# Last stage: first logits of the next group ahead of tree 7's masks, LN4's rows a tree earlier, and GpSimd makes LN3's rows

## The reference, cut to what matters

```python
x = x + _L0_xattn_ref(_layernorm(x), ctx, W, b)
x = x + _L0_ffn_ref(_layernorm(x), ...)          # shared part + one expert of 8 per token
x = x + _L1_xattn_ref(_layernorm(x), ctx, ctx, Wq, bq, Wk, bk, Wv, bv)     # LN3
x = x + _L1_ffn_ref(_layernorm(x), W_in, b_in, W_out)                      # LN4

def _L1_ffn_ref(oldx, W_in, b_in, W_out):        # 8 trees of 255 nodes
    logits = x @ W_in.T + b_in
    decisions = logits > 0
    acts = silu(logits)
    # from the root, the decision at each node picks one of its two children, 7 levels deep
    # dmap is 1 at the 8 nodes on that path, 0 elsewhere
    return (acts * dmap) @ W_out.T
```

## Time and profile before

| | us |
|---|---|
| median of 3 runs | 847.22 (845.65 to 848.89) |
| the profiled execution | 849.45 |
| its span, first to last instruction | 847.6 |
| third stage in it | from 365.8 to the end |
| TensorE busy | 787.2 (93%) |
| VectorE busy | 655.7 (77%) |
| ScalarE busy | 541.6 (64%) |
| GpSimd busy | 265.4 (31%) |

### The profile page before, as it was taken

One profiled execution on the slowest core, in us unless ns is written; L12 is line 12 of the kernel. 1 busy time (PEld: TensorE's weight loads), 2 busy tenths in 40 slices (PEclk: granted clock), 3 DMA queues, 4 the chain that ended last, 5 costly groups with the idle time before them and its releaser, 6 DMA issues.

```text
span 847.6 us, 15269 instructions
## 1 busy us (share of the span) xinstructions
PE 787.2 (93%) x4452; PEld 633.5 (75%) x4493; DVE 655.7 (77%) x1742; ACT 541.6 (64%) x948; POOL 265.4 (31%) x308
## 2 busy tenths in 40 slices
PE   5899998987878998999999999999999999999997
PEld 4788776776768898977777777777777777777775
DVE  5888889787844456768988887888888788888774
ACT  3577667565322334366877777777777777778765
POOL 2333222887287143112320321232132133111000
PEclk9999999999999999999999999999999999999999
DMA  6346784742334343100000000000000000000000
GB/s 170 89 137 191 194 221 130 202 130 85 87 108 149 95 116 91 51 26 13 26 23 4 25 25 0 25 25 19 6 25 25 0 25 25 11 14 14 14 1 25
DMA packets 91428, 55.88 MB, mean 66 GB/s; under 512 B 13439, under 2 KB 88055, under 8 KB 91255
## 3 DMA queue, kind: packets, MB, share of 16 engines
q1 hardware_dynamic: 75440, 41.29, 17.4%
q0 software_dynamic: 4096, 8.40, 3.5%
q10 hardware_dynamic: 11847, 5.64, 2.4%
HBM read 32.23 MB, written 23.07 MB: 65 GB/s over the span
## 4 chain that ended last, share of the span: by engine, by line
PE 41%; DVE 28%; issue 12%; ACT 12%; POOL 3%; another core or an unknown queue 2%; DVEq 1%; DMA 0%; ACTq 0%; POOLq 0%; SPq 0%
PE PS L823 7%; PE PS L808 6%; DVE sil_l L1522 4%; DVE dec L1506 3%; DVE xn_c L1149 3%; PE PS L1009 3%; PE PS L1068 3%; PE PS L1069 3%; PE PS L1070 3%; ACT sil L765 3%; DVE xn L1149 2%; PE PS L1090 2%; PE PS L1092 2%; PE PS L1091 2%; DVE st L1138 2%
## 5 line engine op out<-in xcount | busy, mean ns | idle before, releaser
L765 ACT ACTIVATE sil<-PS,b_in_c 128x512 f32<-128x512 f32 x256 | 162.3, 686 | 113.6 <-PE PS L1077 71.3
L1522 DVE TENSOR_TENSOR sil_l<-sil,sil_h 128x512 fp32r<-128x512 f32 x256 | 164.8, 685 | 44.7 <-ACT sil_h L773 44.3
L526 POOL TENSOR_TENSOR ve<-mv,eps 128x4 f32<-128x4 f32 x64 | 19.2, 300 | 450.2 <-DVE mv L1143 450.1
L773 ACT ACTIVATE sil_h<-sil 128x512 fp32r<-128x512 f32 x224 | 128.9, 631 | 0.0
L1090 PE MATMUL PS<-sil_h,wout_l 128*128 128x512 f32 x256 | 117.8, 460 | 1.6 <-DVE sil_l L1522 1.6
L1506 DVE TENSOR_SCALAR dec<-PS,b_in_c 128x512 bf16<-128x512 f32 x128 | 95.6, 747 | 26.1 <-PE PS L1070 24.3
L1068 PE MATMUL PS<-x4T_h,win_l 128*128 128x512 f32 x256 | 102.2, 399 | 1.6 <-ACT yo L725 0.7
L1092 PE MATMUL PS<-sil_h,wout_h 128*128 128x512 f32 x256 | 100.8, 394 | 0.0
L1091 PE MATMUL PS<-sil_l,wout_h 128*128 128x512 f32 x256 | 100.3, 392 | 0.0
L1069 PE MATMUL PS<-x4T_l,win_h 128*128 128x512 f32 x256 | 100.0, 390 | 0.0
L1070 PE MATMUL PS<-x4T_h,win_h 128*128 128x512 f32 x256 | 99.8, 390 | 0.0
(11 more groups left out here) (169 smaller groups left out, 1549.6 us busy)
## 6 DMA issues: line engine op xcount, KB each, us to landing
x_sorted<-zeros SPq DMA_DIRECT2D x4, 1280.0 KB, 6.8
xs_in<-x_sorted SPq DMA_DIRECT2D x20, 256.0 KB
y_sorted<-yo ACTq DMA_DIRECT2D x20, 256.0 KB
X<-in_x SPq DMA_DIRECT2D x16, 256.0 KB
rows<-xn SPq DMA_DIRECT2D x16, 256.0 KB
out<-res SPq DMA_DIRECT2D x16, 256.0 KB
ctxT<-in_ctx_t SPq DMA_DIRECT2D x16, 240.0 KB
ctx_rows<-in_ctx_kv SPq DMA_DIRECT2D x16, 240.0 KB
```

The lines of the kernel that those rows point to most:

```text
L765: act.activation(tile(sil[p % 2], c, W), bank(2 * (p % 2) + c), ACT.Silu, bias=b_in_c[:, 2 * p + c:2 * p + c + 1]).then_inc(t_silu, 1)
L773: act.activation(tile(sil_h[p % 2], c, W), tile(sil[p % 2], c, W), ACT.Copy).then_inc(t_hi, 1)
L1522: dve.tensor_tensor(tile(sil_l[p % 2], c, W), tile(sil[p % 2], c, W), tile(sil_h[p % 2], c, W).bitcast(F32), ALU.subtract).then_inc(t_lo, 1)
```

## The change

On TensorE the next group's first logits stand where tree 7 had no logits to issue, ahead of tree 7's masks, and the turns of LN4's rows move from p = 7 to p = 6, behind tree 7's logits. ScalarE's high part of x4 and VectorE's low part move from 7 to 6 with them, `c_stats4` from 5 to 4 (right behind `c_attended`), `c_norm4` from 6 to 5. VectorE's `c_add_routed` and `c_norm3` of groups 2 to 15 are gone; GpSimd adds the routed rows as one 128 x 512 operation and makes LN3's rows as two, a subtraction and a multiplication with the mean and the factor broadcast over 128 columns, with a semaphore between them. GpSimd's gather moves ahead of `rstd(0, g+2)` and behind the addition, its loops are written out, and `c_stats3` waits for LN3's rows of the group before.

```diff
+            def add_routed(h, u):
+                pool.wait_ge(y_in[u], 16 * G * (h // 2 + 1))
+                row = cols(X, h * W, W)
+                pool.tensor_tensor(row, row, ys[u], ALU.add).then_inc(c_x2, 1)
+
+            def norm3(h):
+                pool.wait_ge(c_rs3, h + 1)
+                pool.wait_ge(c_x4T_ps, h - 1)
+                rows, dst = by_tile(cols(X, h * W, W)), by_tile(xn_c)
+                pool.tensor_tensor(dst, rows, mv[:, 0, :, 0:1].to_broadcast([P, G, P]), ALU.subtract).then_inc(c_mid3, 1)
+                pool.wait_ge(c_mid3, h - 1)
+                pool.tensor_tensor(dst, dst, rs[:, 0, :].unsqueeze(2).to_broadcast([P, G, P]),
+                                   ALU.mult).then_inc(c_xn3, 1)
+
             def c_body(g, u, half):
                 if not last(g, 2):
+                    add_routed(g + 2, u)
+                    if not last(g, 3):
+                        pool.wait_ge(c_x2, g + 2)
+                        gather(g + 3, 1 - u, half)
                     rstd(0, g + 2, c_mv3, c_ve3, c_rs3)
-                    if not last(g, 3):
-                        gather(g + 3, 1 - u, half)
+                    norm3(g + 2)
                 if not last(g, 1):
                     rstd(1, g + 1, c_mv4, c_ve4, c_rs4)
-            c_body(0, 0, 0)
-            with pool.Fori(0, HG // 2 - 2) as i:
...
+            for g in range(NG):
+                c_body(g, g % 2, 0 if g + 3 < HG else 1)
...
-                    if p == 7 and not last(g, 1):
+                    if p == 6 and not last(g, 1):
                         c_x4_high(g + 1)
...
                     if p + 1 < TREES:
                         t_logits(g, p + 1)
-                    if p == 7 and not last(g, 1):
+                    elif not last(g, 1):
+                        t_logits(g + 1, 0)
+                    if p == 6 and not last(g, 1):
                         c_turn_x4(g + 1)
                     t_path(g, p)
...
-                    if p == TREES - 1 and not last(g, 1):
-                        t_logits(g + 1, 0)
...
             def c_stats3(h):
                 dve.wait_ge(c_x2, h + 1)
+                if not below(h, 2):
+                    dve.wait_ge(c_xn3, h)
                 stats(0, h, c_st3, c_mv3)
...
+                    if p == 6 and not last(g, 1):
+                        c_x4_low(g + 1)
                     if p + 1 < TREES:
                         t_decide(g, p + 1)
                     elif not last(g, 1):
-                        c_x4_low(g + 1)
                         t_decide(g + 1, 0)
...
                         if p == 4:
                             c_attended(g + 1)
+                            c_stats4(g + 1)
                         if p == 5:
-                            c_stats4(g + 1)
-                        if p == 6:
                             c_norm4(g + 1)
                     if not last(g, 2):
-                        if p == 0:
-                            c_add_routed(g + 2, u)
                         if p == 2:
                             c_stats3(g + 2)
-                        if p == 3:
-                            c_norm3(g + 2)
```

More of the change, by code:

```diff
@@ L275, in program @@
             "r_xT_ps", "r_xT", "r_w", "r_gu_ps", "r_sg", "r_act", "r_y_ps", "r_y"))
-        y_in, stored = sems("y_in", 2), sems("stored", 2)
+        y_in, stored, c_mid3 = sems("y_in", 2), sems("stored", 2), sem("c_mid3")
         (c_idx, c_x2, c_st3, c_mv3, c_ve3, c_rs3, c_xn3, c_xnT_ps, c_xnT, c_s_ps, c_max, c_shift, c_exp,
```

## The result

| | before | after |
|---|---|---|
| median, in the comparison on one chip | 847.41 us (845.65 to 848.89) | 860.56 us (857.61 to 861.52) |
| ratio after / before | | 1.0142, 95% interval 1.0122 to 1.0161 |
| profiled execution, and its span | 849.45, 847.6 | 860.16, 858.1 |
| third stage: first logits matmul to the end | 481.8 | 858.1 - 364.5 = 493.6 |

What follows compares the result with a forecast made beforehand. TensorE was taken to pace the last stage, busy 469.5 of 481.8 us. 13 groups at 0.2 + 0.25 + 0.85 - 0.4 = +0.9, with the last groups +11.4, gave 858.6 us against the median; range 844 to 867.

Steps and rivals of the forecast that it cites:

- Earlier x4: Last stage, load before x4's turns: turning a tree sooner removes TensorE's wait for LN4's rows, gaining 0.4 us a group.
- Collision 1: At tree 3: GpSimd's LN3 subtraction gets between tree 2's two low parts on VectorE; TensorE loses 0.2 us a group.
- Collision 2: At tree 4: LN4's statistics now precede tree 4's low parts, which come late for TensorE; 0.25 us lost a group.
- Collision 3: At tree 6: GpSimd's routed-rows addition holds up LN4's normalising, so x4's turns start late; 0.85 us lost a group.
- Sum: Last stage: losses less the gain make +0.9 us for each of 13 groups; +11.4 us together with the last groups.
- No collision bites: Rival for the last stage: LN4's rows complete before tree 7's logits end, only the gain remains; 841.2 us, chance 0.15.
- only the addition collides: Rival: tree 2's low parts stay together, only LN4's rows are late; +0.25 us for 13 groups, 849.7 us, chance 0.2.
- More than the three: Rival: index copy also gets between LN4's normalising operations, 0.3 to 0.6 us more for 13 groups; 863 to 867 us, chance 0.07.
- as at 171 us: Place in before's trace: four normalising operations beside GpSimd's scaling took 2.06 us instead of 1.12, ending 0.86 after it.
- The port: SBUF port shared by VectorE and GpSimd: each new GpSimd operation shuts out low parts and normalising for about a microsecond.
- would hardly fall: Sign for the forecast: VectorE's busy time in the last stage stays nearly level despite 1.8 us a group less work.

Runs made afterwards that it cites:

- e4_placed: Changed kernel with GpSimd's addition waiting for tree 2's decision, LN3's subtraction for tree 3's low parts, gather ahead of the addition; ratio to before 0.9972.
- e5_placed_first: As e4_placed, but in the first group the addition stands ahead of the gather; ratio to before 0.9954.
- e1_order_only: Changed kernel's new order kept, but the routed rows' addition and LN3's rows back on VectorE; ratio to before 1.0046.
- e6_old_order: e5_placed_first's GpSimd work with TensorE, VectorE and ScalarE in the order of before; ratio to before 0.9985.
- e2_add_back: Changed kernel with only the routed rows' addition given back to VectorE; ratio to before 1.0050.
- e9_after_rows: Changed kernel with one wait more, so GpSimd's addition starts after LN4's rows are written; ratio to before 1.0024.
- e8_write_added: Kernel before plus an unneeded GpSimd memset of 128 x 1024 behind each reciprocal root; single run 842.35 against 840.99 us.
- e7_read_added: Kernel before plus an unneeded GpSimd addition of 128 x 512 behind each reciprocal root; single run 868.24 against 840.99 us.

## Why the prediction was right

The instants that the prediction worked out, moved by the 4.88 us that lie between tree 2's low parts before (587.80) and after (592.68), against what the trace of after shows in the two timelines above:

| step | predicted | measured |
|---|---|---|
| subtraction starts | 592.95 | 592.98 |
| subtraction ends, between the low parts | 594.28 | 594.28 |
| tree 2's second low part ends | 594.83 | 594.82 |
| tree 3's low parts start | 596.03 | 596.00 |
| tree 4's low parts start | 601.43 | 601.46 |
| addition starts | 603.58 | 603.56 |
| LN4's rows done | 605.73 | 605.73 |
| TensorE through tree 7's logits | 604.92 | 605.05 |
| x4's turns start | 605.78 | 605.78 |

- **Earlier x4, -0.4 a group.** A group takes 29.6 us in e4_placed and e5_placed_first, which have the new order and neither collision 1 nor 3, against 29.9. That is 0.3, and tree 4's output still loses 0.08 a group there on average, so the gain itself is about 0.4; 5.1 / 15 = 0.34 of it is the wait that goes. e1_order_only and e6_old_order showed what I had left out: the order and the relief of VectorE gain it only together.
- **Collision 1, 0.2 a group.** The hold is 0.21, and with the slower restart of TensorE 0.32. Over the stage 2.5 / 13 = 0.19; the first group has none. Right, but for the restart, which I had not counted.
- **Collision 2, 0.25 a group.** It is 602.17 - 601.95 = 0.22 in this group, and 0.12 and 0.22 in turn in the middle groups, so a little over-sized: the low parts come when I said, but TensorE wants them at 601.95 and not at 596.8 + 0.2 + 4.88 = 601.88, because of the restart at tree 2. The 3.8 us of the stage hold 0.70 in the first group and 0.56 in the last one with a successor, where I had none.
- **Collision 3, 0.85 a group.** 605.78 - 605.05 = 0.73. VectorE's side came to the hundredth; TensorE was there 0.13 later than I had it: it had lost 605.05 - (599.59 + 4.88) = 0.58 by then and not 0.45, 0.32 of it at tree 2 and 0.22 at tree 4. In after, LN4's four operations take 2.01 to 2.03 us in all 13 groups behind which an addition stands and 1.12 in the two that have none. e2_add_back and e9_after_rows confirm place and cause, by taking the operation away and by moving it.
- **Sum, +0.9 a group.** Losses of 0.32 + 0.22 + 0.73 = 1.27 and a gain of 0.4 make +0.9, which is the distance of 30.8 from 29.9. 13 such groups give 11.7, and the stage grew by 11.8. The mechanism held, but that the sum fits to a tenth is luck: the sizes that I missed by 0.1 cancel, and the first group and the last two are not as I had them either.
- **No collision bites; only the addition collides.** Both are out: tree 2's low parts and LN4's rows, which they needed at their usual length, took 2.14 and 2.03 us. **More than the three**: the index copy starts at 604.82 in GpSimd's queue and the four operations end 0.86 after the addition, as at 171 us; the first of the four ends 0.09 after it and the others follow at 0.26 each, their usual step, so nothing slipped in.
- **The port.** LN4's rows end 0.86 us after GpSimd's addition, as at 171 us, and the second low part 0.54 after the subtraction (594.82 - 594.28), against my 0.55. The multiplication (594.35 to 595.72) held neither the decision nor the result that VectorE reads out of PSUM beside it: 0.74 and 0.67 us, against 0.75 and 0.68 in before. By the Trainium skill (SBUF — State Buffer, Who interferes with whom) a blocked instruction would start in full after the release, 1.12 us before its end; the trace doesn't agree. The same section lists casts among the operations that can use the shared pair, and says that an operation with two SBUF inputs meets GpSimd's reads and not an operation that only writes. The casts of e4_placed and the low parts of e8_write_added agree with it.

VectorE's busy time "would hardly fall": it rose by 3.1 us. The profiled execution came to 860.2 us where the sum said 860.8.

Open: which engine goes first when both want the port. In after the subtraction, 0.30 us behind the first low part, went ahead of the second; in e9_after_rows the addition, 0.16 us behind it, had to wait for both. In e7_read_added one 0.18 us behind got in between. Over all groups of e9_after_rows it is always so: 13 of 13 subtractions get in at tree 2, 13 of 13 additions wait at tree 5. So it is neither chance nor the start offset. In the timelines shown, VectorE idled for 1.18 us ahead of tree 2's low parts and came to tree 5's straight from LN4's rows; whether that decides was not tried.

## What to carry to other kernels

Work that is moved to GpSimd to relieve VectorE is not free beside it: an operation of 128 x 512 with SBUF inputs holds normalising, casts and two-input operations for about its own length. So look up in the timeline what VectorE runs at that instant, and tie the GpSimd operation by a semaphore to a stretch in which VectorE reads PSUM; here the same instructions gave 1.0142 without that and 0.9954 with it. And an order change that removes one wait should be tried together with the relief that it needs, and alone: here each alone gave 1.0046 and 0.9985.

## What was not expected of the hardware

- A weight load that was held costs more than the hold: the matmul behind it is followed after 0.34 us instead of 0.23 (594.88 to 595.22).
- A GpSimd addition can be the one that is held: 2.28 us instead of 1.29 in e9_after_rows.
- A memset of 0.94 us delayed four normalising operations by 0.35 us (1.46 - 1.11), although 0.79 of it still lay ahead when they began: the first two end together, 0.09 and 0.15 us after it. It did not delay low parts.
- The first indirect transfer behind the addition took GpSimd 2.06 us to issue in after, at 605.80, beside tree 5's low parts; the same one takes 1.06 in e5_placed_first at 618.33, also beside tree 5's low parts, so what lengthens it stays open. The mean over the kernel went from 1090 to 1284 ns (in the pages of before and after). It delayed nothing here.
